# Attention in cycles of two key tiles: scores of both, both pairs of row-maximum passes, both weighted sums

## The reference

```python
qg = x @ Wq;  q, gate = qg[..., :512], qg[..., 512:]
k, v = x @ Wk, x @ Wv                       # 2 heads of 64
q, k = partial_rope(q), partial_rope(k)     # the first 16 of 64 channels
scores = einsum('bkgsd,bktd->bkgst', q, k) / 8
attn = softmax(scores)                      # over 2048 keys
out = einsum('bkgst,bktd->bkgsd', attn, v) * silu(gate)
x = layernorm(x + out @ Wo)
h = bitlinear(x, w_fc) + g * (x @ v_lr.T @ fast_b.T @ u.T)
x = layernorm(x + bitlinear(relu(h)**2, w_proj))
```

## Time and profile before

| | |
|---|---|
| median of three runs | 1774.87 us |
| the profiled execution: its time | 1773.95 us |
| the profiled execution: span from first to last instruction | 1772.1 us |
| mean granted clock of TensorE in it | 0.976 of full speed |
| attention of the first batch | from about 92 to about 775 us |
| attention of the second batch | from about 959 to about 1640 us |

### The profile page before, as it was taken

The page is one execution under the profiler, slowest core; times in us unless marked ns, Lnnn a source line. Parts: engine busy times, 40 slices in busy tenths (PEclk is TensorE's granted clock), DMA queues, the critical chain, the costliest instruction groups (busy, mean ns, idle before and its releaser), DMA issues.

```text
span 1772.1 us, 24588 instructions
## 1 busy us (share of the span) xinstructions
PE 1674.5 (94%) x6902; PEld 858.6 (48%) x6902; DVE 1378.8 (78%) x1692; ACT 710.5 (40%) x895; POOL 1030.5 (58%) x765
## 2 busy tenths in 40 slices
PE   5699999999999999999878999999999999999996
PEld 3444444444444444447744444444444444444685
DVE  6678888878887787757767778888888888886587
ACT  1234444444444443444332444444444444444352
POOL 0556666666666665654344666666666666657342
PEclk9789999999999999999887999999999999999998
DMA  4600001111111100020043000010000000000001
GB/s 163 160 14 23 23 23 25 24 26 27 27 24 24 25 20 1 1 77 25 25 115 82 23 23 23 23 24 23 22 22 23 22 22 22 19 1 1 24 25 48
DMA packets 36906, 59.68 MB, mean 34 GB/s; under 512 B 6624, under 2 KB 17264, under 8 KB 36288
## 3 DMA queue, kind: packets, MB, share of 16 engines
q1 hardware_dynamic: 36800, 58.50, 12.6%
HBM read 20.07 MB, written 4.19 MB: 14 GB/s over the span
## 4 chain that ended last, share of the span: by engine, by line
PE 75%; DVE 12%; issue 7%; POOL 3%; DMA 2%; ACT 1%; SPq 0%; DVEq 0%; POOLq 0%; ACTq 0%
PE ob L568 23%; PE sc L553 14%; PE sc L556 11%; PE mx L526 11%; PE misc L506 6%; PE mx L665 3%; DVE acc L323 2%; DVE maxp L1040 2%; POOL acc L323 2%; PE misc L579 1%; DVE maxp L1178 1%; PE sc L632 1%; PE ob L680 1%; DMA acc<-in_x 1%; DVE oge L1069 1%
## 5 line engine op out<-in xcount | busy, mean ns | idle before, releaser
L323 POOL TENSOR_TENSOR acc<-acc,probs 128x512 f32<-128x512 f32 x448 | 602.8, 1346 | 365.8 <-DVE acc L323 353.4
L1040 DVE TENSOR_REDUCE maxp<-mx 128x2 f32<-128x1024 f32 x468 | 567.1, 1212 | 232.3 <-PE mx L528 225.8
L820 ACT ACTIVATE probs<-sc 128x1024 f32<-128x1024 f32 x512 | 501.2, 1025 | 574.5 <-PE sc L556 574.5
L568 PE MATMUL ob<-probs,v_sb 128*64 128x512 f32 x2048 | 496.3, 605 | 0.5 <-ACT probs L820 0.5
L323 DVE TENSOR_TENSOR acc<-acc,probs 128x512 f32<-128x512 f32 x448 | 422.8, 944 | 23.5 <-ACT probs L820 22.6
L553 PE MATMUL sc<-qa,kab 128*128 128x512 f32 x1024 | 351.1, 424 | 0.0
L556 PE MATMUL sc<-qb,kab 128*128 128x512 f32 x1024 | 320.8, 394 | 0.0
L526 PE MATMUL mx<-kab,qa 64*128 64x512 f32 x490 | 248.4, 507 | 32.3 <-DMA kab<-high_sb 12.4
L528 PE MATMUL mx<-kab,qa 64*128 64x512 f32 x490 | 247.9, 506 | 0.0
L526 PEld LDWEIGHTS mx<-kab,qa 64*128 64x128 f32 x490 | 91.1, 186 | 295.3 <-issue 153.1
L568 PEld LDWEIGHTS ob<-probs,v_sb 128*64 128x64 f32 x2048 | 124.0, 136 | 212.6 <-issue 149.7
(11 more groups left out here) (130 smaller groups left out, 1549.0 us busy)
## 6 DMA issues: line engine op xcount, KB each, us to landing
qa<-high_sb SPq DMA_DIRECT2D x128, 128.0 KB, 2.3
qb<-low_sb SPq DMA_DIRECT2D x64, 128.0 KB, 2.3
tables_sb<-in_tables SPq DMA_DIRECT2D x34, 128.0 KB, 2.4
xT_sb<-in_xT SPq DMA_DIRECT2D x2, 2048.0 KB, 9.4
acc<-in_x SPq DMA_DIRECT2D x8, 512.0 KB, 4.1
out_y<-acc SPq DMA_DIRECT2D x8, 512.0 KB, 3.2
kab<-acc SPq DMA_DIRECT2D x24, 128.0 KB, 2.4
rot_sb<-raw_sb SPq DMA_DIRECT2D x72, 32.0 KB, 1.8
```

Source lines behind the costliest of these rows:

```text
L323: ops.tensor_tensor(total, total, part, ALU.add).then_inc(summed, 1)
L568: mm = nc.tensor.matmul(ob[hd * D:(hd + 1) * D, :], v_sb[:, t, kv * D:(kv + 1) * D], probs[:, k % RING, hd * CHUNK:(hd + 1) * CHUNK], star ...
L820: nc.scalar.activation(probs[:, k % RING, :].rearrange("p (h n) -> p h n", h=2), sc[:, 2 * (k % 2):2 * (k % 2) + 2, :], ACT.Exp, scale=flo ...
L1040: nc.vector.tensor_reduce(two_columns(p, j), mx[:, :, :], AX_X, ALU.max).then_inc(maxed, 1)
```

## The change

The walk over the steps becomes a walk over *cycles* of two key tiles (index `y`, eight a unit). In a cycle PE does the scores of tiles 2y+2 and 2y+3 (eight matmuls), then side work, then both passes of row maxima, then the weighted sums of tiles 2y and 2y+1.

The banks of PSUM are dealt anew. The four banks of `sc` now hold two row-maximum passes, so a pass waits for the reduction before the last one. The scores go into `trio`, three banks (the two of `mx` and `misc` before) that half tiles, one head each, take in turn: the even tile's heads into banks 0 and 1, the odd tile's into 2 and 0. Bank 1 is also the bank of the side work (`side`), which waits for the exponential that reads bank 1.

The exponential of a tile is split into two of 128x512, one per head, each with its own count on `scores_ready` and `probs_ready`. The second head's scores of an odd tile wait for the exponential of the first head of the even tile just before.

On DVE the reciprocals move to the ends of cycles 1 to 4. On POOL the rope products go between the running sums of tiles 6 and 7, the rope sum after that of tile 7, the gating of the unit before goes after the sum of tile 9, and the last rope step after that of tile 11. On SP the row maxima are placed before the new queries.

```diff
-        mx = ps("mx", [P, 2, CHUNK])
+        trio = ps("trio", [P, 3, CHUNK])
...
-        misc = ps("misc", [P, CHUNK])
+        mx = trio[:, 0:2, :]
+        side = trio[:, 1, :]
+        misc = trio[:, 2, :]
...
-        MAX_PAIRS = [mx[:, :, :], sc[:, 2:4, :]]
+        MAX_PAIRS = [sc[:, 0:2, :], sc[:, 2:4, :]]
+
+        def score_bank(k, hd):
+
+            return trio[:, (2 * (k % 2) + hd) % 3, :]
...
-                pe.wait_ge(maxed, done(unit * PASSES + j))
-                pass_of_two_heads(mx, p % PAIRS, j).then_inc(max_ready, 1)
+                pe.wait_ge(maxed, done(unit * PASSES + j - 1))
+                pass_of_two_heads(MAX_PAIRS[j % 2], p % PAIRS, j).then_inc(max_ready, 1)
...
-                pe.wait_ge(probs_ready, done(n - 1))
+                if t % 2 == 0:
+                    pe.wait_ge(probs_ready, done(2 * n))
                 for hd in range(2):
...
+                    if t % 2 == 0 and hd == 1 and side_free is not None:
+                        pe.wait_ge(side_free[0], side_free[1])
+                    if t % 2 and hd == 1:
+                        pe.wait_ge(probs_ready, done(2 * n - 1))
+                    bank = score_bank(t, hd)
+                    nc.tensor.matmul(bank, ka[:, kv, keys], qa[:, p % PAIRS, hd, :], start=True, stop=False)
+                    nc.tensor.matmul(bank, kb[:, kv, keys], qb[:, p % PAIRS, hd, :], start=False, stop=True)\
+                      .then_inc(scores_ready, 1)
...
+                    for t in range(2 * y + 2, 2 * y + 4):
+                        if t < STEPS:
+                            scores(b, c, p, t, side_free)
+                        elif not last:
+                            scores(b, c, p + 1, t - STEPS, side_free)
+
+                    if (y == 0 and not first(c, p)) or (y == 2 and has_q(c, p)) or (y == 5 and exists(c, p, 1)) or y == 6:
+                        pe.wait_ge(probs_ready, done(2 * (unit * STEPS + 2 * y + 3)))
...
+                    if y == 2 and has_q(c, p):
+                        project(wqg_sb, (p + AHEAD) % PAIRS * P, c + (p + AHEAD) // PAIRS, q_ready, side)
...
+                    look_ahead(LEAD + 2 * y)
+                    look_ahead(LEAD + 2 * y + 1)
+                    weighted_v(b, c, p, 2 * y)
+                    weighted_v(b, c, p, 2 * y + 1)
...
+            def exponential(b, c, p, t):
+
+                n = (b * UNITS + c * PAIRS + p) * STEPS + t
+                for hd in range(2):
+                    act.wait_ge(scores_ready, done(2 * n + hd + 1))
+                    if hd == 0:
+                        act.wait_ge(pv_done, done(n + 1 - RING))
+                        act.wait_ge(sum_a, done(n + 1 - RING))
+                        act.wait_ge(sum_b, done(n + 1 - RING))
+                    nc.scalar.activation(probs[:, t % RING, hd * CHUNK:(hd + 1) * CHUNK], score_bank(t, hd), ACT.Exp,
+                                         scale=float(D) ** -0.5).then_inc(probs_ready, 1)
...
-                    add_exponentials(pool, nc.gpsimd, b, c, k, 0, sum_a, sum_b)
-                    if t == 11 and not first(c, p):
+                    add_exponentials(pool, nc.gpsimd, b, c, p, 2 * y, 0, sum_a, sum_b)
+                    if y == 3 and has_q(c, p):
+                        rope(nc.gpsimd, behind(p, c), b)
+                    add_exponentials(pool, nc.gpsimd, b, c, p, 2 * y + 1, 0, sum_a, sum_b)
+                    if y == 3 and has_q(c, p):
+                        rope_add(nc.gpsimd, behind(p, c), b)
+                    if y == 4 and not first(c, p):
                         gated(b, c, p - 1)
...
-                    look_ahead(LEAD + t)
-                    add_exponentials(dve, nc.vector, b, c, k, 1, sum_b)
...
+                    add_exponentials(dve, nc.vector, b, c, p, 2 * y, 1, sum_b)
...
+                    look_ahead(LEAD + 2 * y)
+                    add_exponentials(dve, nc.vector, b, c, p, 2 * y + 1, 1, sum_b)
+                    look_ahead(LEAD + 2 * y + 1)
+                    if y in RECIP_CYCLES and not first(c, p):
+                        reciprocal(b, c, p - 1, RECIP_CYCLES.index(y))
```

More of the change, by code:

```diff
@@ L583, in step, with emit @@
             def step(b):
[L584 to L585 removed]
+                def emit(c, p, y):
                     unit = b * UNITS + c * PAIRS + p
+                    last = isinstance(c, int) and c == NCH - 1 and p == PAIRS - 1
                     def look_ahead(j):
@@ L617, in emit @@
-                    if t == 13:
-                        if exists(c, p, 1):
-                            pe.wait_ge(m_copied, done(unit + 2))
-                        else:
-                            pe.wait_ge(den_used, done(unit))
-                        project(wqg_sb, HEADS * D + p % PAIRS * P, c, gate_ready)
+                    side_free = None
+                    if y == 1 and not first(c, p):
+                        side_free = (den_used, done(unit))
+                    if y == 3 and has_q(c, p):
+                        side_free = (q_copied, done(b * STAGES + c * PAIRS + PRO + p + 1))
@@ new lines, in emit @@
+                    if y == 0 and not first(c, p):
+                        pe.wait_ge(gate_copied, done(unit))
+                        denominators(b, c, p - 1, side)
+                    if y == 2 and has_q(c, p):
+                        project(wqg_sb, (p + AHEAD) % PAIRS * P, c + (p + AHEAD) // PAIRS, q_ready, side)
+                    if y == 5 and exists(c, p, 1):
+                        max_transpose(b, c, p + 1, side)
+                    if y == 6:
+                        project(wqg_sb, HEADS * D + p % PAIRS * P, c, gate_ready, side)
@@ L786, in copy_stage @@
                 act.wait_ge(low_done[slot], done(uses(stage, b)))
-                bank = FRONT_BANKS[number % 2] if in_front else misc
-                nc.scalar.copy(raw[slot], bank[:, :]).then_inc(q_copied, 1)
+                bank = FRONT_BANKS[number % 2] if in_front else side
+                nc.scalar.copy(raw[slot], bank).then_inc(q_copied, 1)
             def round_stage(stage, b):
@@ L810, in step, with emit @@
             def step(b):
-                def emit(c, k):
-                    p, t = k // STEPS, k % STEPS
+                def emit(c, p, y):
                     unit = b * UNITS + c * PAIRS + p
-                    n = (b * UNITS + c * PAIRS) * STEPS + k
-                    act.wait_ge(scores_ready, done(n + 1))
-                    act.wait_ge(pv_done, done(n + 1 - RING))
-                    act.wait_ge(sum_a, done(n + 1 - RING))
-                    act.wait_ge(sum_b, done(n + 1 - RING))
-                    nc.scalar.activation(probs[:, k % RING, :].rearrange("p (h n) -> p h n", h=2),
-                                         sc[:, 2 * (k % 2):2 * (k % 2) + 2, :], ACT.Exp,
-                                         scale=float(D) ** -0.5).then_inc(probs_ready, 1)
-                    if t == 0 and not first(c, p):
-                        copy_o(b, c, p - 1)
-                    if t == 6 and has_q(c, p):
+                    last = isinstance(c, int) and c == NCH - 1 and p == PAIRS - 1
+                    if y == 0 and not first(c, p):
+                        copy_o(b, c, p - 1)
+                    for t in range(2 * y + 2, 2 * y + 4):
+                        if t < STEPS:
+                            exponential(b, c, p, t)
+                        elif not last:
+                            exponential(b, c, p + 1, t - STEPS)
+                    if y == 2 and has_q(c, p):
@@ L833, in emit @@
+                    if y == 5 and has_q(c, p):
                         round_stage(behind(p, c), b)
```

182 lines of the change are left out of this document (72 added, 110 removed).

## The result

The changed kernel takes 1879.11 us (median of 4 runs, 1871.66 to 1888.27) against 1775.01 before: 1.0588 times as long, interval 1.0566 to 1.0611. I had said 1829 (1780 to 1872): the direction is right, the size is about half, and the time lies above the range. The profiled execution took 1871.66 us, 97.7 more than that of before.

What follows compares the result with a forecast made beforehand. PE, 94% busy, was taken to bound the kernel. 24 units at +2.12 us (50.9) and eight at +0.44 (3.5) gave 1773.95 + 54.4 + 0.9 = 1829 us, range 1780 to 1872.

Steps and rivals of the forecast that it cites:

- POOL chain of cycles 5 and 6: Exponentials wait for POOL's running sums, late behind rope and gating products; PE waits 2.04 us a unit in 24 units.
- score block: First score matmul to first row-maximum pass; new score order and banks costed at nothing, -0.02 to +0.02 us a cycle.
- edges, denominators: PE, per unit: adjacent passes save 8 x -0.09 = -0.72 us; denominators no longer directly after weighted sums lose +0.10.
- row-max wait: PE's wait for DVE's row-maximum reduction vanishes with two bank pairs: -0.38 us a unit.
- round trip, other cycles: Fourth half tile's scores wait for the same cycle's first-half exponential: +0.18 us in each cycle outside 5 and 6.
- long form: On ACT, a wait on an instruction ahead starts the exponential 0.19 us after its scores, not 0.04.
- Increments: 512 more semaphore increments, left out of the sum; the skill's 26.3 ns each would make it 13.5 us higher.
- eight units without rope or gating: Units without the POOL chain: edges, row-maximum wait and eight round trips give +0.44 us each, 3.5 us in all.
- 1: Rival for the whole kernel: POOL is not late, only the round trip counts; +14, 1789 us; chance 0.14.
- 2: Rival for the whole kernel: the round trip is hidden, POOL is late; +26, 1800 us; chance 0.12.
- 4: Rival: contention all the way, each POOL instruction meets a DVE add; +113, 1888 us; chance 0.08.
- rival 3: Both new waits vanish, double-buffered row maxima win; -1.00 x 32, 1743 us; chance 0.09.

Runs made afterwards that it cites:

- e8: e7 with the low part of the rotated queries behind the sum of tile 15 instead of tile 13; 1741.27 us, ratio 0.9818.
- e6: e4 with the wait order of e2, its output not the layer's; 1732.33 us, ratio 0.9759.
- e7: Changed kernel with the edits of e2 and e3, and POOL's rope, gating and low part set one by one between the sums; 1759.95 us, ratio 0.9909.
- e2: Changed kernel with ACT's waits on the sums ahead of its wait on the scores; 1837.83 us, ratio 1.0351.
- e3: Changed kernel with DVE's first sum of a unit ahead of the denominators' fold and the first reduction; 1853.37 us, ratio 1.0437.
- e1: Changed kernel with POOL's gating back after the sum of tile 11, as before the change; 1821.92 us, ratio 1.0252.
- e4: Changed kernel with eight probability buffers instead of four, four in the attention output's memory, so the output is not the layer's; 1762.23 us, ratio 0.9921.
- e5: Changed kernel with the edits of e1, e2 and e3 together; 1779.02 us, ratio 1.0019.

## Why the prediction was wrong, step by step

Two terms of the sum failed. The POOL chain of cycles 5 and 6, priced at 2.04 us a unit, cost 3.23; and the wait of cycle 1, 0.88, stood at nothing. Per steady unit, in us; the measured figures are differences of score blocks or of units against e8, whose cycles wait for nothing but 0.43 in cycle 5 (5.21 us there, 4.78 in e6), so that 42.11 - 0.43 = 41.68 is the unit without waits.

| step | predicted | measured | from |
|---|---|---|---|
| edges, denominators | -0.62 | -1.51 | 41.68 - 43.57 + 0.38 |
| row-max wait | -0.38 | -0.38 | no wait of PE left |
| round trip, other cycles | 6 x 0.18 | 5 x 0.15 | 2.24 - 2.09 |
| cycle 1 | (in the row above) | 0.88 | 2.97 - 2.09 |
| cycles 5 and 6 | 2.04 | 3.23 | 3.23 + 4.00 - 2 x 2.00 |
| sum | 2.12 | 2.97 | unit measured: 2.95 |

My sum lacks 43 us of the 97.7: 24 x 0.83 = 20 in the steady units, 9 of half clock, 15 at the ends of the batches and outside the loop. The steady units alone would have left the time inside the range; the other two, which my sum hardly has, carry it out.

*Edges: right in kind, too small.* I changed only the edge between two passes and left the second pass at 0.43. It takes 0.32 to the weighted sums, which no row of before showed. Without waits the cycle is 4.62 us (e7, 347.32 to 351.94), not 4.68; the rest is at the projections and denominators. The score block, priced at nothing with 0.02 either way, works against this: it takes 2.09 without a wait where it took 2.04.

*Round trip: right.* 0.19 us behind the scores, the long form, and a delay of PE in every cycle; e2 and e6 show the price as 0.15 instead of 0.18.

*Increments: right to leave out.* In the changed kernel every second score matmul of the rows above carries an increment, and the starts stay 0.22 to 0.24 apart. The page "TensorE: Matmul & The Clock Gate" of the Trainium skill (section "The cost: per-tile semaphore tail") has 26.3 ns each in the tail behind small matmuls packed into the array, which the scores are not; this case's traces show nothing of it in the starts on PE.

*Cycle 1: a wait that I did not see.* Rows of the changed kernel around it, one engine after the other:

```profile
331.64 0.69 DVE L1080 SCALAR_TENSOR_TENSOR oge<-oge,trio 128x512 f32<-128x512 f32 x1 [2.39 <-PE trio L586]
332.24 1.22 DVE L1059 TENSOR_REDUCE maxp<-sc 128x2 f32<-128x1024 f32 x1
333.38 0.68 DVE L321 TENSOR_TENSOR acc<-probs 128x512 f32<-128x512 f32 x1
...
334.37 1.29 POOL L321 TENSOR_TENSOR acc<-probs 128x512 f32<-128x512 f32 x1 [4.73 <-DVE acc L321]
...
335.75 2.07 ACT L828 ACTIVATE probs<-trio 128x512 f32<-128x512 f32 x4 [4.48 <-PE trio L564]
...
336.40 0.50 PE L563 MATMUL trio<-qa,kab 128*128 128x512 f32 x1 [0.66 <-ACT probs L828]
```

A unit's first sum adds tiles 0 and 1 in one instruction. So the buffer of tile 0 comes free only with POOL's L321 (334.37 + 1.29 = 335.66), which stands behind DVE's (ends 334.06), which stands behind the denominators' fold and a reduction. The exponential of tile 4 starts at 335.75. I followed the chain for tile 10 and took the others to have more room; e3 moves this one instruction and the wait goes.

*Cycles 5 and 6: right chain, 3.23 instead of 2.04. This is the term that was mis-sized.* POOL of the changed kernel answers to the earlier trace rows, with DVE ahead of it and DVE's adds beside its end:

```profile
344.20 1.23 DVE L1059 TENSOR_REDUCE maxp<-sc 128x2 f32<-128x1024 f32 x1 [2.24 <-PE sc L532]
...
347.94 0.63 DVE L325 TENSOR_TENSOR acc<-acc,probs 128x512 f32<-128x512 f32 x1
...
348.80 1.27 POOL L325 TENSOR_TENSOR acc<-acc,probs 128x512 f32<-128x512 f32 x1 [1.24 <-ACT probs L828]
350.03 1.27 POOL L296 TENSOR_TENSOR raw_sb<-raw_sb,tables_sb 128x512 f32<-128x512 f32 x1
...
355.88 3.20 POOL L325 TENSOR_TENSOR acc<-acc,probs 128x512 f32<-128x512 f32 x2
...
357.74 1.09 ACT L828 ACTIVATE probs<-trio 128x512 f32<-128x512 f32 x2 [2.34 <-POOL acc L325]
...
359.03 1.74 POOL L943 TENSOR_TENSOR oge<-oge 128x512 f32<-128x512 f32 x1
...
360.95 0.68 DVE L325 TENSOR_TENSOR acc<-acc,probs 128x512 f32<-128x512 f32 x1
361.03 1.75 POOL L946 TENSOR_TENSOR og<-oge 128x512 f32 x1 [0.26 <-POOL oge L943]
...
362.68 0.68 DVE L325 TENSOR_TENSOR acc<-acc,probs 128x512 f32<-128x512 f32 x1
362.74 3.17 POOL L325 TENSOR_TENSOR acc<-acc,probs 128x512 f32<-128x512 f32 x2
...
364.56 1.09 ACT L828 ACTIVATE probs<-trio 128x512 f32<-128x512 f32 x2 [3.81 <-POOL acc L325]
```

POOL works from 348.80 to the exponential at 364.56 with one idle of 0.26, as predicted. From the end of the pass ahead of DVE's chain (344.16) to PE's seventh matmul at 365.21 it is 21.05 us where I had 20.27. The 0.78 are, first, a start of POOL 0.23 behind DVE's add (347.94 + 0.63 = 348.57), not 0.04; it is 0.08 in the kernel before (medians 0.08 and 0.24 over the sums that wait for DVE). A likely cause could be read ahead of the result, though no run tried it: the sum itself carried the wait `sum_b` before, and the changed kernel has it on an instruction ahead, the same long form that I priced on ACT and left out here. Second, the second gating product takes 1.75 us here against the 1.27 that I took from the earlier trace rows (mean 1699 ns against 1381 over the 24): a DVE add begins just ahead of it, and again just ahead of the sum behind it. Some 0.1 more is in the sums. Each such sum or product then takes some 1.72 to 1.76, and DVE's add and reduction together take 1.73 (360.95 to 362.68), so the two stay in step. The page "SBUF — State Buffer" of the Trainium skill (section "SBUF: two separate sides") has a DVE operation with two inputs in SBUF and a GpSimd one that reads SBUF take turns, for a whole instruction, at a shared port pair; the 0.45 to 0.49 us are near the 0.52 from the product's start to the next start on DVE (361.03 to 361.55). The other 0.4 are PE's, which the better edges bring to this point sooner: what the edges gain ahead of a fixed chain is waited for again behind it.

*The half clock and the batch ends: hardly in my sum.* The half clock costs nine us in the profiled execution, more in the others (granted clock 0.962 to 0.968 against 0.971). The stretches went with the gating moved (e1) and with the shorter wait in cycle 6 (e2), and stayed where that wait did (e3); that the wait causes them is likely by this, but no run tried it alone. It is not enough by itself: all 24 steady units of the changed kernel have the wait of cycle 6 (1.74 to 1.80 us), and only 5 have a stretch behind it. The waits of cycle 5, some 1.0 us, have none. I had priced the eight units without rope or gating at +0.44 each. The last three intervals of a batch give +7.4 together; there too the first sum waits (0.66 us at 711.84), and the gating alone makes cycle 6 wait (1.10 us at 737.01). In the middle one PE waits 0.62 us (754.79), 1.94 (780.12) and 0.19 (786.25) for exponentials, 2.75 of its 4.7; where the rest lies stays open.

The rivals: 1 and 2 each left out one of the waits that are all there; 4 (1888, every POOL instruction met by an add) is nearest in time, but POOL's first six instructions take 8.9 us as forecast (348.80 to the exponential at 357.74 behind them), and contention is only part of the rest. What rival 3 describes is e4 and e8: with the sums out of the way the new order does win. That e8's 1741 falls on rival 3's 1743 is luck: its edges gain more, and it keeps the wait of cycle 5.

## What to carry to other kernels

When a reorder lets the bounding engine run ahead, follow every chain that frees a buffer, for each place of the ring, and the first one of a loop above all, since that is where instructions differ. On a helper engine count the other instructions between two that someone waits for: POOL is busy for 1043.8 us in the changed kernel and for 1042.3 in the fastest version, which takes 138 us less. Of these the place of POOL's work gave some 95 (57 in e1, 19 from e5 to e7, 19 from e7 to e8), the order of ACT's waits and of DVE's first sum the rest. A gain ahead of such a chain is no gain until the chain is shorter.

## What the runs showed of the hardware

- Two row-maximum passes in sequence, then weighted sums: 0.34 and 0.32 us, against 0.43 for a pass by itself. The edge depends on what stands next to it, also for the second.
- A wait carried by the ACT instruction itself lets it start 0.04 us after its scores, one on an instruction ahead of it 0.19; on POOL, behind DVE's add, it is 0.08 and 0.24. The order of two waits, one of them long passed, was worth 0.15 us in each cycle without another wait, and 29.9 us between e4 and e6.
- PE, 90% busy in all, fell to half its clock (granted clock 0.50, the 1.2 GHz level) for 3.4 us behind a wait of 1.76 us and lost some 1.7 us more. That happened behind 5 of 24 such waits. If the wait is the cause, it cost twice its length there.
- A POOL sum or product of 1.27 us took 1.72 to 1.76 where a DVE add began just ahead of it; in e2, where neither gating product begins behind an add, both take 1.27 to 1.28.
